# Two transposed query tiles in another order, and the keys rounded one unit earlier, in a fused attention and expert kernel

## The reference

```python
def cond(x):        # one expert of 8 per sequence, picked by argmax of cond_8
    return (silu(x @ wu.T + bu) * (x @ wg.T + bg)) @ wd.T + bd
def attn(q):        # 16 heads of width 8
    Q, K, V = q @ Wq.T + bq, q @ Wk.T + bk, q @ Wv.T + bv
    scores = Q K^T / sqrt(8)                       # (b, h, 512, 512)
    scores = conv over keys, 3 taps, mixing the 16 heads, + conv_b
    return softmax(scores) V @ Wo.T + bo
x = x + attn(cond(x))
z = x @ W_base.T + b_base + 2 * lora(x, cond_8)
x = x + ffn(z)      # top-1 of 8 experts, capacity 128 tokens each, 128 -> 512 -> 128
```

## Time and profile before

| | us |
|---|---|
| median of 3 runs (lowest, highest) | 263.36 (263.22, 264.77) |
| the profiled execution, its own time | 265.03 |
| span of the profiled execution | 263.1 |
| TensorE busy in the span | 239.2 (91%) |
| VectorE busy | 209.1 (79%) |
| ScalarE busy | 168.5 (64%) |
| GpSimd busy | 143.0 (54%) |

### The profile page before, as it was taken

The page is one execution under the profiler, slowest core; times in us unless marked ns, Lnnn a source line. Parts: engine busy times, 40 slices in busy tenths (PEclk is TensorE's granted clock), DMA queues, the critical chain, the costliest instruction groups (busy, mean ns, idle before and its releaser), DMA issues.

```text
span 263.1 us, 5532 instructions
## 1 busy us (share of the span) xinstructions
PE 239.2 (91%) x1775; PEld 186.7 (71%) x1775; DVE 209.1 (79%) x509; ACT 168.5 (64%) x307; POOL 143.0 (54%) x166
## 2 busy tenths in 40 slices
PE   7996978989898998999999879799998999999993
PEld 7454856867676776867877757578777876879982
DVE  1549899888979889897987998979979666677553
ACT  2643589967778687787868557778679660214321
POOL 1019779978679787787968446779783000000000
PEclk9999879999999999999999999999999999999998
DMA  6950007456273535637353507163544704400002
GB/s 206 360 232 0 0 4 220 144 120 189 51 226 133 120 122 118 198 99 182 125 120 123 118 31 210 59 183 123 120 165 120 196 4 125 197 0 2 0 2 80
DMA packets 13766, 31.73 MB, mean 121 GB/s; under 512 B 1458, under 2 KB 10674, under 8 KB 13490
## 3 DMA queue, kind: packets, MB, share of 16 engines
q1 hardware_dynamic: 13314, 30.82, 38.9%
q10 hardware_dynamic: 432, 0.65, 0.8%
HBM read 19.14 MB, written 12.32 MB: 120 GB/s over the span
## 4 chain that ended last, share of the span: by engine, by line
PE 62%; DVE 14%; issue 9%; ACT 6%; POOL 4%; DMA 2%; DVEq 1%; SPq 0%; ACTq 0%; POOLq 0%
PE sc L829 8%; PE tp L974 8%; PE sc L831 6%; PE sc L830 6%; PE pvbank L850 6%; PE pvbank L848 5%; DVE Pb L554 5%; PE sc L1060 3%; PE tp L1070 3%; DVE w2s L689 2%; ACT Kh L354 2%; POOL Kl L256 2%; ACT Pb L359 2%; DVE kc L498 2%; PE sc L1020 1%
## 5 line engine op out<-in xcount | busy, mean ns | idle before, releaser
L359 ACT ACTIVATE Pb<-Pb,nbias 128x512 f32<-128x512 f32 x128 | 90.9, 719 | 42.2 <-DVE Pb L554 41.0
L554 DVE TENSOR_SCALAR_CACHE_REDUCE Pb<-sc,col 128x512 f32<-128x512 f32 x128 | 92.0, 738 | 15.1 <-PE sc L831 13.9
L829 PE MATMUL sc<-Kh,Ql 128*128 128x512 f32 x124 | 57.6, 465 | 9.0 <-issue 4.6
L256 POOL TENSOR_TENSOR Kl<-kc,Kh 128x512 fp32r<-128x512 f32 x29 | 37.5, 1292 | 31.0 <-ACT Kh L354 30.3
L974 PE MATMUL tp<-cst,Pb 128*128 128x128 f32 x332 | 50.3, 275 | 4.1 <-ACT PT L406 4.0
L974 PEld LDWEIGHTS tp<-cst,Pb 128*128 128x128 f32 x332 | 40.5, 141 | 17.4 <-issue 4.9
L831 PE MATMUL sc<-Kh,Qh 128*128 128x512 f32 x124 | 49.3, 398 | 0.0
L830 PE MATMUL sc<-Kl,Qh 128*128 128x512 f32 x124 | 49.3, 397 | 0.0
L406 ACT ACTIVATE PT<-tp 128x512 f32<-128x512 f32 x79 | 46.0, 582 | 1.2 <-PE tp L974 1.2
L268 POOL TENSOR_TENSOR td<-ta,tc_ 128x512 f32<-128x512 f32 x31 | 41.2, 1329 | 2.6
L261 POOL TENSOR_SCALAR ta<-Kp,cwS 128x512 f32<-128x512 f32 x31 | 30.5, 983 | 16.0 <-ACT Kp L332 15.9
(11 more groups left out here) (241 smaller groups left out, 305.7 us busy)
## 6 DMA issues: line engine op xcount, KB each, us to landing
swap<-w2s SPq DMA_DIRECT2D x15, 768.0 KB, 3.3
PT<-swap SPq DMA_DIRECT2D x60, 192.0 KB, 3.9
w1s<-in_w SPq DMA_DIRECT2D x1, 2048.0 KB, 10.6
w2s<-in_w SPq DMA_DIRECT2D x1, 2048.0 KB, 7.9
cst<-in_consts SPq DMA_DIRECT2D x1, 648.0 KB, 6.2
xTs<-in_xT SPq DMA_DIRECT2D x2, 256.0 KB, 3.5
we<-in_wexp SPq DMA_DIRECT2D x2, 256.0 KB, 4.0
b2s<-in_b2row SPq DMA_DIRECT2D x1, 512.0 KB, 11.4
```

The costliest lines, as they stand in the source:

```text
L256: pool.tensor_tensor(Kl[:, n, :], kc[:, n, :], Kh[:, n, :].bitcast(f32), ALU.subtract)\
L359: act.activation(Pb[:, k, :], Pb[:, k, :], ACT.Exp, bias=nbias[:, k:k + 1], scale=-1.0)\
L554: dve.tensor_scalar(Pb[:, k, :], SC[k % 4][:, :], cb, None, ALU.subtract, ALU.min, accum_out=nbias[:, k:k + 1]).then_inc(s["mx"], 1)
L829: pe.matmul(SC[k][:, :], ql, Kh[:, h2, :], start=True, stop=False)
```

## The change

A table `TILE` gives the query tile of each of a pair's eight units, (0, 1, 3, 2) in the first head and (1, 0, 3, 2) in the second. The three block tiles stay tiles 0 and 2 of the first head and tile 0 of the second, and stand now in units 0, 3 and 5 instead of 0, 2 and 4. TensorE transposes units 1, 2, 4, 6 and 7 instead of 1, 3, 5, 6 and 7. The last pair keeps its order. No instruction is added or removed. Separately, `high_half` of a head's keys moves on ScalarE one unit up: from the first unit of a head (`u % 4 == 0`) to the last unit of the head before (`u % 4 == 3`), behind the exponential there. Head 2, the first that this concerns, is rounded ahead of unit 0.

```diff
+TILE = (0, 1, 3, 2, 1, 0, 3, 2)
...
         def by_blocks(b, g, u):
-            return u % 8 in (0, 2, 4) and not last_pair(b, g, u)
+            return u % 8 in (0, 3, 5) and not last_pair(b, g, u)
+
+        def tile_of(b, g, u):
+            return u % QT if last_pair(b, g, u) else TILE[u % 8]
...
-            at = u % 8
-            return 10 * (NG * b + g) + 5 * (u // 8) + (at // 2 if at % 2 == 0 or at < 7 or last_pair(b, g, u) else 4)
+            at = u % 8 // 2 if last_pair(b, g, u) else (None, 0, 1, None, 2, None, 3, 4)[u % 8]
+            return 10 * (NG * b + g) + 5 * (u // 8) + at
...
-                if u % QT == 0 and (not isinstance(g, int) or hd + 2 < B * H):
-                    high_half(hd + 2, (u // QT) % 2)
+                if u % QT == 3 and (not isinstance(g, int) or hd + 3 < B * H):
+                    high_half(hd + 3, (u // QT + 1) % 2)
...
             for k in range(AHEAD):
                 exp(k, k)
+            high_half(2, 0)
             for u in range(TURN):
...
-                half_tile, w = u % QT // 2, u // (2 * QT)
+                half_tile, w = tile_of(b, g, u) // 2, u // (2 * QT)
...
-                if q == 0:
+                if u % QT == 0:
                     pe.wait_ge(s["hi"], hd + 1)
                     pe.wait_ge(s["lo"], hd)
```

More of the change, by code:

```diff
@@ L181, in by_blocks @@
         def by_blocks(b, g, u):
-            return u % 8 in (0, 2, 4) and not last_pair(b, g, u)
+            return u % 8 in (0, 3, 5) and not last_pair(b, g, u)
+        def tile_of(b, g, u):
+            return u % QT if last_pair(b, g, u) else TILE[u % 8]
         def by_pe(b, g, u):
-            at = u % 8
-            return 10 * (NG * b + g) + 5 * (u // 8) + (at // 2 if at % 2 == 0 or at < 7 or last_pair(b, g, u) else 4)
+            at = u % 8 // 2 if last_pair(b, g, u) else (None, 0, 1, None, 2, None, 3, 4)[u % 8]
+            return 10 * (NG * b + g) + 5 * (u // 8) + at
         def nth_blocks(b, g, u):
-            return 6 * (NG * b + g) + 3 * (u // 8) + u % 8 // 2
+            return 6 * (NG * b + g) + 3 * (u // 8) + (0, 3, 5).index(u % 8)
         @block.sync
@@ L397, in unit @@
                     after(0, AT_ACT[g, u])
-                if u % 2 == 1 or u % 8 == 6 and not last_pair(b, g, u):
+                if u % 2 == 1 if last_pair(b, g, u) else not by_blocks(b, g, u):
                     nth = by_pe(b, g, u)
                     bank = TP[1 if last_pair(b, g, u) else by_pe(0, 0, u) % 2]
-                    half_tile = u % QT // 2
-                    dst = PTA[:, u // QT % G, :, half_tile * 128:(half_tile + 1) * 128] if u % 2 else \
+                    half_tile, parity = divmod(tile_of(b, g, u), 2)
+                    dst = PTA[:, u // QT % G, :, half_tile * 128:(half_tile + 1) * 128] if parity else \
                         PTC[:, u // 8, :, :]
@@ L818, in _, with scores @@
             project(1)
-            def scores(n, hd, b, u):
-                k, q = u % 4, u % QT
+            def scores(n, hd, b, u, q):
+                k = u % 4
                 qh, ql = Qh[:, b, q * 128:(q + 1) * 128], Ql[:, b, q * 128:(q + 1) * 128]
                 h2 = (u // QT) % 2
-                if q == 0:
+                if u % QT == 0:
                     pe.wait_ge(s["hi"], hd + 1)
@@ L958, in unit @@
                     over = isinstance(g, int) and G * g + m // QT >= H
-                    scores(n + AHEAD, H * b + G * g + m // QT, b + 1 if over else b, m)
+                    scores(n + AHEAD, H * b + G * g + m // QT, b + 1 if over else b, m,
+                           m % QT if m < U and last_pair(b, g, m) else TILE[m % 8])
                 if not by_blocks(b, g, u):
@@ L992, in _ @@
                     pe.wait_ge(s["vev"], 1)
-                qh, ql = Qh[:, 0, k * 128:(k + 1) * 128], Ql[:, 0, k * 128:(k + 1) * 128]
+                at = slice(TILE[k] * 128, (TILE[k] + 1) * 128)
+                qh, ql = Qh[:, 0, at], Ql[:, 0, at]
                 pe.matmul(SC[k][:, :], ql, Kh[:, 0, :], start=True, stop=False)
```

## The result

| | before | after |
|---|---|---|
| median, us (runs) | 264.06 (4) | 252.99 (4) |
| lowest, highest | 263.22, 265.10 | 252.45, 253.40 |
| profiled execution, its own time and span | 265.03, 263.1 | 252.98, 251.0 |

The ratio is 0.958, 95% interval 0.953 to 0.962: 11 us faster, against the 9 of the sum. Before's median is of one run more than the one ahead of the prediction.

A forecast was written before the change was run, and what follows sets the result against it. TensorE was taken to bound the kernel, needing 20.2 of 22.5 us a group. Terms -3.5 - 6.7 - 1.2 + 2.4 gave -9.0, so 263.4 became 254.4 us, range 251.0 to 260.5.

The forecast's parts named there:

- the sum: Whole kernel: waits removed, -3.5 - 6.7 - 1.2, plus 2.4 of new waits, give -9.0 us; no instruction comes or goes.
- What bounds the kernel: Whole kernel: TensorE sets the pace, needing 20.2 of 22.5 us in each group of 16 units.
- The keys: First scores of a head: TensorE's waits for `Kl`, partly shown as "issue", vanish with the earlier rounding, -6.7 us.
- The evictions: Transposes of a pair's unit 7: five waits of TensorE for ScalarE's evictions all go, -3.5 us.
- the third head: First scores of head 2: its rounding starts 1.2 us earlier and the rest of the chain follows, -1.2 us.
- What is late next: All groups: TensorE, VectorE and GpSimd, now close, make each other wait 0.3 us a group, +2.4 over 8 groups.
- The transfers: A pair's third block turn, one unit later: its transfers stay hidden with 2 us left; late transfers had chance 0.05.
- Only the order counts: Rival at the heads: GpSimd itself is the chain, `Kl` comes no earlier and 6.7 stays; 258.7 us, chance 0.18.
- The slower one: Rival on VectorE: `kc` runs into GpSimd's work and lengthens, up to 1.69 us each; 265.8 us, chance 0.05.
- The waits move: Rival in each unit: VectorE's minima become the release of TensorE's scores; 262.2 us, no change, chance 0.10.
- The marks: Signs in the changed trace: group 21.0 to 21.5 us, GpSimd's rounding wait under 12, TensorE's head waits near nothing.

## Why the prediction was right, step by step

**What bounds the kernel** held. TensorE's own work was put at 20.2 us a group; a group now lasts 20.3, with TensorE busy throughout.

**The keys** (-6.7) held in size only together with the order. The waits at the heads went in the changed kernel to 1.4 us under `Kl`, but in the kernel with early keys alone they went too, to 1.7, and the time did not move. The term was read as if the wait that is seen were the only one in that place. A second chain, over unit 2's turn and keys, the exponentials and the eviction of unit 5, ended just behind it, and its wait was small because TensorE was already late from the head.

**The evictions** (-3.5): alone, the order gave 5.4, and beside early keys 10. So the step that failed is the sum itself, "the sum is thus one of waits", taken as if each edit owned its waits: nothing for the keys alone and 5.4 for the order alone, but 11 together. In the changed kernel 2.2 us of such waits are left, 1.7 of them outside the last pair (0.88 at 39.69, 0.79 at 71.12), where the prediction had none.

**The sum** of -9.0 is near the measured -11.1 partly by luck, as its terms missed on both sides. By the waits that the traces name between the fifth head and the last pair, 5.7 of the 6.7 us of the keys went; the 1.02 at the fifth head stayed, as 1.39. Of the 3.5 for evictions 2.7 went, and the third head gave nothing. Against that, the +2.4 was not there, the waits in the routing steps shrank by 0.5, and TensorE's starts show 2.6 us more gain than its named waits: the gaps that are wider than their waits, for which the prediction had 1 us in its range and nothing in its sum.

**The third head** (-1.2) was right in its place, 33.63 against the forecast 33.9, and wrong in the sum: head 2 rounded late costs nothing in the end, since the fourth head starts no earlier.

**What is late next** (+2.4) was mis-sized: nothing of it was there, as in plain groups TensorE has no wait left. VectorE does not come closer: its busy time fell from 19.9 to 18.8 a group, and `kc` took 0.99 us on the mean against 1.08 before (30.6 us in 31, and 33.5 in 31). In the two groups shown, `kc` makes 0.8 us of the 1.0 to 1.1 of the fall. The keys meet GpSimd at another place now: before, 20 of the 31 started during a low half and took 1.12 us on the mean, in the change 2 did, and 21 started during the shorter `ta` and `tc_`, at 0.86 and 0.94. The shorter mean goes with the early rounding, not with the order: it is 0.92 with the keys alone and 1.16 with the order alone.

**The transfers** were put down as hidden, "with 2 us left". They were hidden in this trace, but with less. From the landing of a pair's last transfer to the first product that uses it there were 2.4 to 9.2 us before, and 4.5 in the pair that the prediction read. In the change that pair has 1.5, and the smallest are 0.2, 0.3 and 0.4. The same kernel, run again, has this:

```profile
183.87 0.38 PE L855 MATMUL pvbank<-PT,Vst 128*32 128x256 f32 x1 [0.99 <-ACT PT L410]
```

The eviction named had ended at 183.38; the transfer landed at 183.78, so it was the transfer that ended this wait. By these margins the transfers stand closest behind TensorE now; no run here tests what a shorter way would give.

**The rivals.** "Only the order counts" named 258.7; the kernel with the order alone took 258.1, but the change was not that case. The slower one needed a mean `kc` of 1.57; it went the other way. It was also reckoned from the median of 0.89, while VectorE's 19.9 us hold the mean of 1.08: from that, the turning point is 1.08 + 2.7 / 4 = 1.76, and even `kc`s of 1.69 throughout would have left VectorE at 22.3 us, under the 22.6 of a group. "The waits move" is what happened in the kernel with early keys alone, to evictions, not to minima.

**The marks.** The group was to be 21.0 to 21.5 us long and is 20.3. GpSimd's wait for roundings was to fall under 12 us and is 19.2: TensorE no longer waits behind it, and GpSimd, with 18.1 to 18.6 us of work in 20.3, simply has time left. That mark was badly chosen. The one that told was TensorE's wait at the heads.

## What to carry to other kernels

A wait in front of an instruction is the distance to the last of several chains; what removing it gives is the distance to the next one, and the next one's own wait can look small only because everything behind the first is already late. Before two edits that each remove one wait are costed as a sum, follow both chains back to the engine that set them, and try each edit alone: here one alone gave nothing, the other 5.4 us, both 11. What was hidden before has less room afterwards: here the transfers' 4.5 us became 1.5. In an order written out by hand, look for the unit where two optional jobs of one engine meet, and for runs of jobs that share two buffers.

## What the runs showed of the hardware

In its first scores, after TensorE has stood 2.17 us, a kernel runs at one of two granted clocks, and that is part of its spread. The stretch from 24 to 29 us in the changed kernel, and in the one with the earlier `diag` step, whose instructions there are the same:

```profile
24.00:29.00 5.00, 4.54 (x14) 3.62 (x15) 4.06 (x8) 2.08 (x3) 4.77 (x6) 0.66 0.00 0
```

```profile
24.00:29.00 5.00, 3.94 (x18) 3.11 (x19) 5.00 (x12) 2.98 (x5) 4.77 (x6) 1.00 0.00 0
```

In the first, a matmul of 128x512 starts each 0.43 us from 24.82 to 27.81, the level of 1.2 GHz; in the second each 0.23, that of 2.4. The fifth head's scores began at 45.85 in the first and 43.46 in the second, and the profiled times are 252.98 and 251.33. In the kernel with the earlier `diag` step the runs at a mean clock of 0.998 and 1.000 took 251.3 and 250.6 us, those at 0.992 took 253.5 and 253.8. Run again, this kernel showed the low level too: 0.69 in the same stretch and the fifth head at 46.02. It is not all of the spread: the six runs of the change run again lie between 251.1 and 254.5 us, all at mean clocks of 0.989 to 0.992. The Trainium skill, TensorE: Matmul & The Clock Gate, section "Part 1: The HAM clock gate", describes such a clock, low until TensorE has been kept busy; the trace agrees with its two levels, the 0.43 and 0.23 us. Why the same stand of 2.17 us lowers it in one run and not in another, no run here shows. It also fell behind the stand of 2.30 us in the kernel with turns in 1, 3, 5, to 0.53, and not behind those of 1.26 us in the change.
